# Down products of two expert pairs in one group, and the last tile's outputs in parts of three tokens and two

## What is computed

```python
# layer 0
scores = x @ Wg.T + bg;  top 2;  p = softmax(top 2)
out = sum_e p_e * (relu(x @ W1[e].T + b1[e]) @ W2[e].T + b2[e])      # hidden width 256
# layer 1
probs = softmax(x @ router_w.T);  top 2, divided by the sum of the two
out = sum_e weight_e * ((silu(x @ w1[e].T) * (x @ w3[e].T)) @ w2[e].T)  # hidden width 170
h = h + out
```

## Time and profile before

| what | us |
|---|---|
| median of 3 runs (1093.0 to 1104.26) | 1102.91 |
| the profiled execution | 1097.99 |
| its span, first to last instruction | 1096.2 |
| PE busy in it | 1004.6 |
| DVE busy | 808.0 |
| ACT busy | 580.6 |
| POOL busy | 399.7 |

### The profile page before, as it was taken

How to read it: one execution, slowest core, us unless ns; L and a number is a source line. 1 busy time by engine, 2 the same in 40 slices (tenths; PEclk the granted TensorE clock), 3 DMA queues, 4 the chain that set the end, 5 groups by cost and what they waited for, 6 DMA issues and landing times. The chain is left out here.

```text
span 1096.2 us, 23392 instructions
## 1 busy us (share of the span) xinstructions
PE 1004.6 (92%) x8389; PEld 720.9 (66%) x8389; DVE 808.0 (74%) x1982; ACT 580.6 (53%) x1331; POOL 399.7 (36%) x391
## 2 busy tenths in 40 slices
PE   5798889879999999998988799988999999999997
PEld 2476766557677767775765577755777777777774
DVE  2595968967766776777777589866877778777775
ACT  2275646565565656564338666765444444444441
POOL 3233602312433343333357568710133333333333
PEclk9899999999999999999999989999999999999999
DMA  8300000003223222322001000000122221221122
GB/s 227 136 2 1 2 2 1 1 12 87 49 51 82 66 50 51 84 63 50 1 19 49 7 2 2 2 3 0 51 65 71 71 65 55 56 55 56 55 56 68
DMA packets 76423, 50.16 MB, mean 46 GB/s; under 512 B 4196, under 2 KB 75124, under 8 KB 75924
## 3 DMA queue, kind: packets, MB, share of 16 engines
q1 hardware_dynamic: 75972, 44.59, 15.8%
q0 software_dynamic: 336, 4.07, 0.9%
HBM read 45.99 MB, written 2.66 MB: 44 GB/s over the span
## 5 line engine op out<-in xcount | busy, mean ns | idle before, releaser
L1579 PE MATMUL moe_psU<-moe_nT_parts,moe_w_hi 128*128 128x320 f32 x988 | 322.6, 338 | 14.1 <-DVE moe_hid L1483 8.8
L1579 PE MATMUL moe_psU<-moe_nT_parts,moe_w_lo 128*128 128x320 f32 x988 | 294.1, 308 | 0.0
L1579 PEld LDWEIGHTS moe_psU<-moe_nT_parts,moe_w_hi 128*128 128x128 f32 x988 | 185.6, 188 | 71.7 <-issue 42.4
L1225 ACT ACTIVATE moe_hid<-moe_psU,middle 128x320 f32<-128x320 f32 x312 | 149.6, 528 | 99.3 <-PE moe_psU L1579 97.7
L1220 ACT ACTIVATE moe_silu<-moe_psU 128x320 f32<-128x320 f32 x286 | 123.9, 439 | 139.2 <-PE moe_psU L1579 112.1
L1579 PEld LDWEIGHTS moe_psU<-moe_nT_parts,moe_w_lo 128*128 128x128 f32 x988 | 186.3, 189 | 0.7 <-issue 0.7
L1483 DVE TENSOR_TENSOR moe_hid<-moe_psU,moe_silu 128x320 f32<-128x320 f32 x286 | 131.3, 485 | 34.4 <-ACT moe_silu L1220 27.6
L1111 POOL TENSOR_TENSOR moe_y_sum<-moe_y_sum,moe_y 128x320 f32<-128x320 f32 x96 | 81.7, 872 | 145.7 <-DVE moe_y L1444 82.1
L1594 PE MATMUL moe_psY<-moe_hid,late 128*64 128x320 f32 x800 | 118.7, 439 | 0.0
L1594 PE MATMUL moe_psY<-moe_hid,middle 128*64 128x320 f32 x800 | 118.6, 439 | 0.0
L139 POOL TENSOR_TENSOR moe_stats<-moe_stats,minus_half 128x5 f32<-128x5 f32 x26 | 30.5, 1171 | 186.3 <-DVE moe_stats L1326 186.3
(11 more groups left out here) (367 smaller groups left out, 1901.3 us busy)
## 6 DMA issues: line engine op xcount, KB each, us to landing
moe_share<-shares SPq DMA_DIRECT2D x208, 160.0 KB, 4.5
images<-in_x SPq DMA_DIRECT2D x8, 576.0 KB, 11.4
late<-in_late POOLq DMA_DIRECT2D x1, 2263.5 KB, 11.3
out_tokens<-h SPq DMA_DIRECT2D x13, 160.0 KB, 1.8
middle<-in_middle POOLq DMA_DIRECT2D x1, 1554.0 KB, 7.1
project_turns<-in_turns SPq DMA_DIRECT2D x8, 160.0 KB, 2.2
early<-in_early SPq DMA_DIRECT2D x1, 1043.0 KB, 18.9
turns_first<-in_turns SPq DMA_DIRECT2D x4, 160.0 KB, 2.3
```

What stands on the lines that cost most here:

```text
L1225: act.activation(hid[hid_of(g, u)][:, :], psU[u % 4][:, 0:HALF], ACT.Relu, bias=late[:, c["b1"]][:, k:k + 1]).then_inc(hid_act, 1)
L1579: last = pe.matmul(psum[:, 0:HALF], w[:, col:col + SPLIT], moving, start=(part == 0), stop=(part == 1))
```

## The change

The hidden tiles get 640 columns (both halves of a chunk in one tile), so that a down product is no longer bound to the half: a pair's output is cut by tokens into parts of 384 and 256 columns (even pairs) or 256 and 384 (odd pairs). `psY` becomes three banks; the even pair lies at columns 128 to 767, the odd one at 768 to 1407, the turned shares at 1408. The bank comes from `psM` in layer 0 (now one bank) and from the gate banks in layer 1 (now two, `u % 2`). The down products of pairs 0 and 1 form one group, those of 2 and 3 another, after (0, 4) and (2, 4) in layer 0 and (0, 1) and (2, 1) in layer 1; DVE weighs the two pairs one after the other. Layer 0 turns in 4 + 1 as layer 1 does, its shares turn at (3, 6) rather than (2, 6), and DVE evicts 12 of its 32 units, not 8. The slots of the small steps move to the two groups. The psM waits on the shares go. In the ending pairs 0 and 1 form a group, pair 2 goes to psU, and pair 3's parts are weighed, summed, turned and added part by part.

```diff
-        on_dve = [(u - first_of[units[u][0]]) in (2, 6) for u in range(UPG)]
+        on_dve = [(u - 5) % 16 in (2, 5, 7, 10, 12, 15) for u in range(UPG)]
...
-        gate_bank = [u % 3 if u < first_of[2] + 2 else (u - 1) % 3 for u in range(UPG)]
+        silu_of = [u % 3 if u < first_of[2] + 2 else (u - 1) % 3 for u in range(UPG)]
...
-        hid = [sb(f"hid{k}", [128, HALF]) for k in range(NHID)]
+        hid = [sb(f"hid{k}", [128, TOK]) for k in range(NHID)]
...
-        psU = [ps(f"psU{k}", 128, HALF) for k in range(4 if layer == 0 else 5)]
-        psY_both = ps("psY", 128, 1024)
-        psY = psY_both[:, :].rearrange("p (x n) -> p x n", x=2)[:, :, 0:HALF]
-        MBANKS = 2 - layer
-        psM = ps("psM", 128, MBANKS * 512)
+        psU = [ps(f"psU{k}", 128, HALF) for k in range(4)]
+        psY = ps("psY", 128, 1536)
+        EVEN_AT, ODD_AT, SHARES_AT = 128, 768, 1408
+        psM = ps("psM", 128, 512)
...
-        TURNS = [(0, T)] if layer == 0 else [(0, 4), (4, T)]
+        TURNS = [(0, 4), (4, T)]
...
-            if last and p % 2:
-                return [psU[half][:, 0:HALF] for half in range(2)]
-            return [psY[:, half, :] for half in range(2)]
+            if last and p == 2:
+                return [(half * HALF, (half + 1) * HALF, psU[half][:, 0:HALF]) for half in range(2)]
+            at, middle = (ODD_AT, 2 * B) if p % 2 and not last or p == 1 else (EVEN_AT, 3 * B)
+            return [(0, middle, psY[:, at:at + middle]), (middle, TOK, psY[:, at + middle:at + TOK])]
...
+        OUTS, READS = [(1, 0), (1, 3)], [(1, 1), (1, 4)]
         if layer == 0:
-            LOGITS, DOWN = (0, 2), 4
-            OUTS, READS = [(1, 0)], [(1, 1)]
-            SHARES, SHARES_READ = (2, 6), (2, 7)
-            TURN, KEEP = [(3, 2)], [(3, 2)]
-            HI, EXP = (1, 5), (2, 3)
+            LOGITS, DOWNS = (0, 2), [(0, 4), (2, 4)]
+            SHARES, SHARES_READ = (3, 6), (3, 7)
+            TURN, KEEP = [(3, 2), (3, 4)], [(3, 2), (3, 4)]
+            HI, EXP = (2, 4), (2, 5)
-            LAST_SLOTS = {(0, 7): "ss", (1, 1): "sssss", (1, 7): "sssss", (2, 1): "mmm", (2, 7): "mmm", (3, 3): "s"}
-            SLOTS = {(0, 4): "aaaannnn", (1, 0): "n", (1, 2): "n", (1, 4): "aaaaan", (1, 7): "aa", (2, 1): "aaa", (2, 4): "neeeeee"}
+            LAST_SLOTS = {(0, 7): "ss", (1, 1): "sssss", (1, 7): "sssss", (3, 0): "mmm", (3, 2): "mmm", (3, 5): "s"}
+            SLOTS = {(0, 4): "nnnnnnaaa", (1, 0): "aa", (1, 3): "aa", (1, 6): "a", (2, 4): "naaaaaan",
+                     (2, 7): "ee", (3, 1): "ee", (3, 3): "ee"}
         else:
-            LOGITS, DOWN = (0, 0), 1
+            LOGITS, DOWNS = (0, 0), [(0, 1), (2, 1)]
...
-            SLOTS = {(0, 1): "aaaannn", (0, 4): "ee", (1, 1): "neeeeeee", (1, 4): "eee", (2, 1): "neeeeeee"}
+            SLOTS = {(0, 1): "aaaannneeeeee", (1, 1): "ne", (1, 4): "ee", (2, 1): "neeeeeeeeeee"}
...
-                    for p in (2, 3):
-                        weigh(j, p, True)
-                        dve.wait_ge(weighed, j * PAIRS + (p + 1))
-                        dve.wait_ge(summed, j * SUMS + (p - 1))
-                        dve.tensor_tensor(y_sum[:, :], y_sum[:, :], y[:, p, :], ALU.add).then_inc(summed, 1)
+                    weigh(j, 2, True)
+                    dve.wait_ge(weighed, j * PAIRS + 3)
+                    dve.wait_ge(summed, j * SUMS + 1)
+                    dve.tensor_tensor(y_sum[:, :], y_sum[:, :], y[:, 2, :], ALU.add).then_inc(summed, 1)
+                    dve.wait_ge(share_in[3], 32 * (j + 1))
+                    dve.wait_ge(summed, j * SUMS + 2)
+                    for part, (t0, t1, psum) in enumerate(outputs_ps(3, True)):
+                        if part == 0:
+                            dve.wait_ge(down_first, 1)
+                        else:
+                            dve.wait_ge(down_mm, (j + 1) * PAIRS)
+                        into, by = y[:, 3, t0:t1], share[:, 3, t0:t1]
...
+                        ins.then_inc(part_weighed, 1)
+                        dve.wait_ge(part_weighed, part + 1)
+                        dve.tensor_tensor(y_sum[:, t0:t1], y_sum[:, t0:t1], into, ALU.add).then_inc(part_summed, 1)
...
-                        if g and k == DOWN:
+                        if g and (p, k) in DOWNS:
                             weigh(g - 1, p)
+                            weigh(g - 1, p + 1)
...
                         if kind == 1:
-                            before = [v for v in range(u) if gate_bank[v] == gate_bank[u]]
-                            wait_evicted(pe, g, before[-1] if before else
-                                         max(v for v in range(UPG) if gate_bank[v] == gate_bank[u]) - UPG)
+                            wait_evicted(pe, g, u - 2)
...
+                def down_part(j, p, part, last=False):
+
                     w = late[:, down_cols].rearrange("p (n d) -> p n d", d=D)
+                    t0, t1, psum = outputs_ps(p, last)[part]
+                    for side, chunk, block_at, start, stop in downs(p):
+                        ins = pe.matmul(psum[64 * side:64 * side + 64, :], w[:, block_at, :], hid[hid_at(j, chunk)][:, t0:t1],
                                         start=start, stop=stop)
+                    return ins
+
+                def down_two(j, p):
+
+                    need(pe, weighed, j * PAIRS + p)
+                    pe.wait_ge(shares_set, j + 1)
+                    down_ready(j, p + 1)
+                    down_part(j, p, 0)
+                    down_part(j, p, 1)
+                    down_part(j, p + 1, 0).then_inc(down_mm, 1)
+                    down_part(j, p + 1, 1).then_inc(down_mm, 1)
...
-                down(NT - 1, 0, True)
-                pe.wait_ge(shares_set, NT)
+                down_two(NT - 1, 0)
                 for part in range(PARTS):
                     turn_out(NT - 2, part)
-                for p in range(1, PAIRS):
-                    down(NT - 1, p, True)
+                for p in (2, 3):
+                    down_last(NT - 1, p)
...
-                turn_out(NT - 1, 0, True)
+                for part in range(PARTS):
+                    turn_out(NT - 1, part, True)
```

More of the change, by code:

```diff
@@ L996, in downs @@
     def downs(p):
-        for half in range(2):
-            for j in range(2):
-                for s in range(2):
-                    e = 2 * p + s
-                    if layer == 0:
-                        yield half, s, unit_of[half, 2 * e + j], 2 * e + j, j == 0, j == 1
-                    else:
-                        yield half, s, unit_of[half, e if j == 0 else E + e // 3], 4 * p + 2 * j + s, j == 0, j == 1
+        for j in range(2):
+            for s in range(2):
+                e = 2 * p + s
+                if layer == 0:
+                    yield s, 2 * e + j, 2 * e + j, j == 0, j == 1
+                else:
+                    yield s, e if j == 0 else E + e // 3, 4 * p + 2 * j + s, j == 0, j == 1
     with ExitStack() as ctx:
@@ L1216, in evict @@
                         act.wait_ge(up_mm, g * UPG + (u + 1))
-                        bank = gate_bank[u]
-                        before = [v for v in range(u) if gate_bank[v] == bank]
-                        wait_evicted(act, g, before[-1] if before else max(v for v in range(UPG) if gate_bank[v] == bank) - UPG)
-                        act.activation(sil[bank][:, :], psU[u % 2][:, 0:HALF], ACT.Silu).then_inc(hid_act, 1)
+                        at = silu_of[u]
+                        before = [v for v in range(u) if silu_of[v] == at]
+                        wait_evicted(act, g, before[-1] if before else max(v for v in range(UPG) if silu_of[v] == at) - UPG)
+                        act.activation(sil[at][:, :], psU[u % 2][:, 0:HALF], ACT.Silu).then_inc(hid_act, 1)
                     elif not on_dve[u]:
@@ L1434, in weigh @@
                     need(dve, summed, (j - 1) * SUMS + max(p, 1) if j else 0)
-                    if last and p % 2:
-                        turns = [(psum, slice(half * HALF, half * HALF + HALF)) for half, psum in enumerate(outputs_ps(p, last))]
-                    else:
-                        turns = [(psY, slice(0, TOK))]
-                    for psum, cols in turns:
-                        into, by = y[:, p, cols], share[:, p, cols]
-                        if len(turns) == 1:
-                            into, by = (x.rearrange("d (x n) -> d x n", x=2) for x in (into, by))
+                    turns = outputs_ps(p, last)
+                    if not (last and p == 2):
+                        at = ODD_AT if p % 2 and not last or p == 1 else EVEN_AT
+                        turns = [(0, TOK, psY[:, at:at + TOK])]
+                    for t0, t1, psum in turns:
+                        into, by = y[:, p, t0:t1], share[:, p, t0:t1]
                         if layer == 0:
@@ L1561, in up @@
                     moving = nTr[g % 2][:, half * HALF:(half + 1) * HALF]
-                    if u == 0 or layer == 1 and half == 1 and units[u - 1][1] == 0:
```

(11 more changed lines are left out.)

110 lines of the change are left out of this document (64 added, 46 removed).

## The result

The changed kernel takes 1144.47 us (median of 4 runs, 1136.72 to 1147.88) beside 1102.55 for the kernel before: ratio 1.0389, interval 1.0306 to 1.0472. It is slower by 42 us where I forecast 1094, 9 us faster, and lies above my range of 1079 to 1107. The profiled execution took 1147.22 us, its span is 1145.4. Ratios are made of fast runs alone, so one run of `l0_old` further down (1619.21 us, granted clock 0.555), the one of that kernel that was traced, counts in none.

The account below looks back on a forecast made before the run. TensorE, busy 92% of the span, was taken as the bound. Terms -35.4 + 13.8 + 15.6 + 3 + 0.5 - 1.35 = -3.9 us on the profiled 1097.99 gave 1094 us; range 1079 to 1107.

Parts of the forecast that it names:

- Groups: Both layers' down products: two groups a tile in place of four save 0.35 us a merge, -16.6 us.
- Rival D: Down groups: merging saves nothing because the drain is paid per pair anyway, +16.6 us, 1111; chance 0.03.
- shares later: Layer 0: weighing waits for later-turned shares, covering the turn's wait; with the transposes 1.3 us a tile, +15.6 us.
- rival B: Layer 0's first weighing: shares land at 9.4 us after the copy, +18 us, 1112; chance 0.09.
- Transposes: Layer 0: the fifth transpose waits for ScalarE's copy of the first four, 0.36 us with the load.
- The old stalls: Both expert layers: routing steps hidden behind down products remove earlier stalls, -7.8 us in layer 0, -11.0 in layer 1.
- The term +13.8: Layer 1: two gate banks in place of three make PE wait for evictions, 1.15 us a tile, +13.8 us.
- Last tile of layer 0: Preparing steps without cover, +0.5 us, ends -1 and 2; the prediction wrote this term for layer 1's last tile.
- First tiles: First tiles of both layers, without down groups: DVE's grouped steps block, together +3 us, ends 0 and 7.
- Tail: Layer 1's end: last weighing to last sum takes about 2.5 us in place of 3.84, -1.35 us.

Follow-up runs that it names:

- l0_old: The changed kernel with layer 0's expert stage taken from the kernel before; 1103.69 us, ratio 1.005 to the kernel before.
- no_idle: The changed kernel with the idle product after (1,4) of layer 0 issued only in the first tile; 1136.23 us, ratio 1.0362.
- const_share: `no_idle` with layer 0 weighing with weight columns in place of shares, not waiting for transfers, in all tiles but the last; 1115.06 us, ratio 1.0147.
- pool_half: `no_idle` with GpSimd adding only the first 320 of 640 columns of each pair in layer 0; 1127.52 us, ratio 1.0279.
- const_spaced: `const_share` with layer 0's second turn moved from (1,3) to (1,6) and its second transposes from (3,4) to (3,6); ratio 1.0186.
- gate2: The kernel before with layer 1's gate banks cut from three to two; 1122.98 us, ratio 1.0213.
- m_back: `no_idle` with all six steps of the next norm at (2,4) in layer 0's last tile; 1131.5 us, ratio 1.0300.

## Why the prediction was wrong

The merges saved what I had said; the steps around them failed. Layer 0's tile was forecast at 21.8 us and took 24.16: an idle product stood in no term, the shares' term was too small, and the old stalls that I took off did not go. The last tile of layer 0 cost 9.1 us for 0.5. Layer 1's tile was forecast at 25.1 and took 25.67. Term by term:

**Groups** (right). A group of 32 passes goes from 423.18 to an up start at 427.63, 4.45 us as forecast. With the low up matmuls on both sides, as in the earlier trace rows, it is 427.88 - 422.94 = 4.94 us less two ups (0.29), 4.65, where two single groups have 2.51 each: 0.37 us a merge is saved. Rival D falls.

**A step never costed: idle products.** The diff makes `DOWNS` a list, and the branch `elif layer == 0 and k == 4 and p < 3` stays. Before it was reached only where there was no group; now (1,4) is no place of a group, so every tile of layer 0 from the second on runs one idle product there, 0.85 us between starts. I read the diff's edits and not what the unchanged branch does under them. The sum put this at nothing; `no_idle` against the changed kernel has 0.63 us a tile at equal landing, 7 us in 11 tiles.

**Term "shares later", +15.6 in layer 0** (mechanism right, size wrong; rival B). Landing came as forecast at its best (8.05 us for 7.9) but at 8.6 in the mean and up to 9.9. My own rule that each microsecond of later landing costs one holds in the tiles (the table under "The idle products"). I took the median landing of all eight transfers, where DVE waits for the fourth in every tile. An estimate by the Trainium skill's fixed cost of about 2 us for a DMA (DMA: Bandwidth & Descriptors, Latency and other measured facts) puts pair 0 in at 4.5 us behind the copy. In the trace its weighing starts 6.4 to 8.2 us behind it, so the measurement decides, and the row was the better guide. I gave 1.3 us a tile to shares, turn and transposes together; `no_idle`'s two stretches are 11.9 and 11.49 us over 9.9 and 10.6 of work, so 2.9. `const_share` prices the shares' part at 1.07 us beyond the turn's wait, plus 5 in the ending. Rival B's 1112 had the place and the direction and a chance of 0.09, which was too little for a place with negative slack already on paper.

**Transposes, 0.36 us.** The stretch from (2,4) lost 0.9. At the transposes themselves PE waits 0.26 (3.1 us in 12). Another 0.22 goes with POOL's adds (`pool_half`). For the remaining 0.4 the profile shows no wait for DVE; one weight load there waits 0.2 for an eviction of ACT. I did not split it.

**The old stalls, -7.8 and -11.0.** In layer 0 they did not go: `const_spaced`, free of shares and turn waits, has 22.07 us against the 21.82 of before. Without any of the new waits the merged order is no shorter. What holds PE there is 0.78 us a tile behind the steps that end the routing, which take longer while POOL adds (the rows of `const_spaced`); behind the two weighings, 1.8 us in a row, its rows show no wait of PE. The other 0.8 over the 20.5 of work is open. In layer 1 the two stretches have 0.97 and 0.68 of stall for 0.7 and 0.4 forecast: 0.5 us a tile, 6 us. The term +13.8 was undersized by that. `gate2` shows that the gate banks and the steps' places belong in one sum, not in two. My -16.6 for the groups is 16.8 by its own factors, which changes nothing.

**Last tile of layer 0, +0.5** (ends -1 and 2): +9.1. I looked for cover on DVE and missed the queue of POOL: the moved norm steps release a deviation, and behind it stand the adds for which the turn waits. Between the ending's (0,4) and (2,4) groups the changed kernel has 13.83 us for 10.39, which is the shares (10.89 in `const_share`); behind them it has 35.57 for 29.93, and of these 5.6 us `m_back` gives 5.0 to 5.4 back.

**First tiles, +3:** +1.0 and +5.6, the sum within my ends of 0 and 7. Of the 5.6 the gate bank has 2.5; my 1.5 stood for bank and steps together. **Tail, -1.35:** layer 1's ending gained 0.5. The rows at the kernel's end show what stands ahead of it now:

```profile
1132.64 0.82 DVE L1452 TENSOR_TENSOR moe_y<-moe_psY,moe_share 128x640 f32<-128x640 f32 x1 [3.21 <-DMA moe_share<-shares]
...
1139.38 0.56 DVE L1476 TENSOR_TENSOR moe_y<-moe_psY,moe_share 128x384 f32<-128x384 f32 x1
...
1141.93 0.60 DVE L1490 TENSOR_TENSOR h<-h,moe_psU 128x128 f32<-128x128 f32 x2
```

From the first part's weighing to the last sum are 1142.53 - 1139.38 = 3.15 us for 3.84, but DVE had waited 3.21 us for pair 0's share a few rows up. Whether that wait costs the 0.85 that is missing was not tried.

The sum by what was measured, in the expert stages: layer 0 tiles 2.3 us each over 11, 25.7, of which idle products 7, the tile at half the clock 1.5 and shares 11.8 (the other 5.4: turn, transposes and what stayed open, less the saved merges); layer 0 ending 9.1; first tiles 6.6; the rest 1.0. Together 42.4.

## What to carry to other kernels

When places become a list, read every unchanged branch that asks for the old places; and for each step that is moved, follow the queue of each engine that it releases, in the last tile too. A transfer that is waited for in every tile is costed by the mean and the spread of its last part, and kernels that wait for it are compared at equal landing; negative slack on paper is a rival of first rank. Merging groups gathers the other engines' work as well: what two groups gave time for in two pieces has to be done in one, and a bank given up for it must be paid from the same sum.

## What was not expected of the hardware

- Some of DVE's steps take longer while POOL adds 128x320: in `no_idle` 0.49 and 0.84 under four adds, in `pool_half`, whose adds ended before, 0.17 and 0.20. Width does not decide it. The normalising product of 128x320 takes 0.48 alone and 1.14 under adds (rows below, adds from 421.02 to 422.70), while the weighing of 128x640 has 0.88 under adds (439.65 in the changed kernel) and 0.88 without (429.45). Nearly all steps that take longer read both inputs from SBUF (the exceptions are two `tensor_scalar` steps); the weighing and the gate product, which read PSUM, and the reciprocals and reductions keep their times in these traces. The two steps of `no_idle` end at 428.37 and 429.25; its four adds end at 429.18.

```profile
259.40 0.48 DVE L1339 TENSOR_TENSOR moe_nrm<-moe_cen,moe_stats 128x320 f32<-128x320 f32 x1
...
421.92 1.14 DVE L1339 TENSOR_TENSOR moe_nrm<-moe_cen,moe_stats 128x320 f32<-128x320 f32 x1
```

- After a stretch in which PE was busy 11.12 of 17 us, the granted clock was 0.52 for the 5 us in which it then worked without a pause, and 1.00 again behind them. Sixteen passes cost 4.54 us for 2.37 there, so a wait of 3.3 us cost more than itself. In the tile at 372 us a wait of 2.61 us did the same, 1.55 us on top.
- Eight transfers of the same size from the same queue landed up to 1.9 us apart from tile to tile (pair 1's weighing starts 8.05 to 9.91 us behind the copy).
